# Gated cross-attention and expert FFN on one core: the context tiles of seven batches turned by DMA transposes instead of TensorE

## The chip, the cores and the metric

The kernel runs on one core of a Trainium2 chip. The metric is the device time of one execution in microseconds. A core has TensorE (PE in the profile; PEld is its weight load), VectorE (DVE), ScalarE (ACT), GpSimd (POOL) and SyncE (SP), each with an instruction queue of its own that it works through in order, and 16 DMA engines. An instruction may wait for a semaphore, and then everything behind it on its engine waits as well.

## The reference

x and the context are 8 batches of 512 tokens by 512 features. A layer norm of x, cross-attention with 8 heads of 64 to the context, an output projection with a gate, and after that a second layer norm and a top-2-of-8 expert FFN:

```
q = (x @ Wq).reshape(B, N, NUM_HEADS, HEAD_DIM)...
k = (context @ Wk)...          v = (context @ Wv)...
attn = softmax(einsum('bhnd,bhmd->bhnm', q, k) * scale)
x = x + tanh(g_xattn[0]) * (einsum('bhnm,bhmd->bhnd', attn, v)... @ Wo + bo)
logits = einsum('bnd,de->bne', layernorm(x), gate_w)   # top 2 of 8 experts
x = x + tanh(g_ffn[0]) * (the two experts' FFN, weighted)
```

## The kernel before, in words

**Splits.** Each fp32 operand of a large product is written as two f16 halves, hi and lo, and a product is three f16 matmuls (hi·hi, hi·lo, lo·hi). ScalarE writes hi, VectorE computes operand minus hi and writes lo.

**Steps.** The main loop has 32 steps, `g = 4 * b + j`: batch b, head pair j. In a step TensorE works on the eight score tiles of pair (b, j) (`scores`, k = 0 to 7), the row maxima of the next pair (`row_max_scores`), the q and k projections of the pair after that (`product` of `qk_parts`), the probabilities times V (`weighted`), and, for the batch before, the transposed head outputs (`oT`), the output projection (`out`), the gate logits and the ranks. ScalarE computes each exponential twice, fp32 into `P32` and f16 into `Ph`; the difference `Pl` is made by VectorE (chunks 0 and 1) and by GpSimd (chunks 2 and 3).

**The tiles of the next batch** are prepared beside it. A batch has four tiles of 128 tokens of x and four of the context. In steps j = 0 and j = 1 two of each are turned: ScalarE normalises x into `xn`; `token_tile` has TensorE transpose the x tile and the context tile, in four 128x128 fp32 transposes each, into PSUM; ScalarE reads the bank and writes hi into `xT` or `cT` (`turned_hi`), VectorE writes lo (`turned_lo`). The first of the two tiles of a step (`side(ahead)`) stands between the transposes of oT and `scores` 6, the second (`side(ahead + 1)`) at the very end of the step. In steps j = 2 and j = 3 `side` is the V projection, which reads `cT`, and the k projections from j = 2 on read it as well. The DMAs that load the tiles of batch b + 2 go out from ScalarE's queue in step j = 2 (`load_tile`).

**PSUM.** `bank_uses` lists all uses of shared banks in order, `bank_places` gives each a place: two banks of `G` in turn, or one of the two banks of `MX`, which otherwise hold the row maxima. A use of `G` waits until the last but one use of `G` has been taken out. The first context tile of each step goes into `MX`, and TensorE waits for `mrow_ready` (the max rows copied out of it) before.

**SyncE's queue** in a step: in batch 0 three loads of FFN weight pieces (`load_piece`); the load of the residual (`load_residual`); `arrange`, twelve DMAs that put q and k into the layout for the scores; `max_rows`, two small DMAs which the next step's first scores wait for; in batch 0 three stores of split pieces (`store_piece`); `turn`, two DMA transposes of the finished second-norm row; `store_x2`. ScalarE and VectorE split the pieces in batch 0 (`piece_hi`, `piece_lo`).

## Time and profile before

| | |
|---|---|
| median of 3 timed runs | 1020.25 us (1018.52 to 1021.1) |
| profiled execution | 1017.04 us, span 1015.3 us |
| TensorE busy | 882.5 us, 87% |
| VectorE, ScalarE, GpSimd busy | 689.9, 568.1, 530.5 us |
| TensorE clock granted, mean | 0.96 of full |

The span is the time from the first to the last instruction of the program; the profiled execution's time lies 1.7 us above it. Busy times are unions of an engine's instructions; a matmul's end is modelled, so the distance between the starts of two matmuls says more than their lengths. In a timeline row, `[0.62 <-DVE tiles L974]` means that the engine stood idle for 0.62 us before this instruction and that VectorE's instruction of line 974, which wrote `tiles`, released it. The main loop runs from 50 us to some 730 us; the expert FFN follows.

### The profile page before, as it was taken

Reading aid. Unit: us, or ns where it says so; the run is one execution under the profiler, and the core shown is the slowest. Engines: PE = TensorE matmul, PEld = TensorE weight load, DVE = VectorE, ACT = ScalarE, POOL = GpSimd, SP = SyncE. Lnnn points to the kernel's source line nnn. Section 1 sums busy time; section 2 is a strip of 40 time slices with the busy share of each in tenths; the row PEclk is TensorE's granted clock in tenths of the full one; section 3 lists DMA queues with packets and bytes.
Section 4 is the critical chain, followed back from the end, with each engine's and each line's share of the span. In section 5 each row is a group of like instructions: output and inputs, shape, how many; then the busy total and the mean of one; then the engine's idle time right before and its main releaser. Section 6 shows DMA issues by size and latency. Waiting matters only on the chain. (4 is left out here: it accounts for less than half of the span.)

```text
span 1015.3 us, 22868 instructions
## 1 busy us (share of the span) xinstructions
PE 882.5 (87%) x8250; PEld 536.1 (53%) x8250; DVE 689.9 (68%) x1612; ACT 568.1 (56%) x1022; POOL 530.5 (52%) x643
## 2 busy tenths in 40 slices
PE   4878999999999999999999999997670899899990
PEld 2334555555555555555555555554340678677770
DVE  5577987677877887787787688688466455345540
ACT  4367766567546656755666665566430466456550
POOL 6222253454466456546545654547754155667765
PEclk9999999999999999999999999999885899999995
DMA  7557834645652354355245433753423589899997
GB/s 264 144 152 225 266 119 123 187 118 116 162 158 73 102 166 109 79 157 164 64 118 151 111 77 95 246 180 95 151 95 136 157 183 206 169 215 213 221 170 100
DMA packets 120509, 153.21 MB, mean 151 GB/s; under 512 B 42960, under 2 KB 75728, under 8 KB 119632
## 3 DMA queue, kind: packets, MB, share of 16 engines
q1 hardware_dynamic: 96624, 101.77, 35.2%
q0 software_dynamic: 16864, 37.40, 18.8%
q10 hardware_dynamic: 6912, 12.59, 4.1%
q8 instruction: 69, 1.13, 0.5%
q14 instruction: 40, 0.33, 0.1%
HBM read 67.06 MB, written 56.56 MB: 122 GB/s over the span
## 5 line engine op out<-in xcount | busy, mean ns | idle before, releaser
L700 POOL TENSOR_TENSOR Pl<-P,Ph 128x512 f16<-128x512 f32 x128 | 152.6, 1203 | 167.5 <-ACT Ph L786 167.0
L783 ACT ACTIVATE P<-ST 128x512 f32<-128x512 f32 x256 | 154.5, 603 | 128.9 <-PE ST L1476 109.2
L984 DVE TENSOR_REDUCE mx<-MX 128x1 f32<-128x512 f32 x256 | 168.7, 685 | 27.9 <-PE MX L1461 27.6
L786 ACT ACTIVATE Ph<-ST 128x512 f16<-128x512 f32 x256 | 155.7, 608 | 1.2 <-remote 0.7
L750 POOL DMA_INDIRECT out_dram<-V,Ph x78 | 121.9, 1563 | 62.2 <-ACT V L938 43.7
L1678 PE MATMUL MX<-heads,tiles 128*128 128x256 f16 x936 | 116.8, 276 | 5.7 <-DVE heads L1359 5.4
L1488 PE MATMUL PV<-V,Ph 128*128 128x65 f16 x1024 | 112.0, 194 | 9.8 <-issue 9.6
L1490 PE MATMUL PV<-V,Ph 128*128 128x64 f16 x1024 | 112.2, 195 | 1.8 <-issue 1.8
L1492 PE MATMUL PV<-V,Pl 128*128 128x65 f16 x1024 | 111.8, 193 | 0.7 <-issue 0.6
L1488 PEld LDWEIGHTS PV<-V,Ph 128*128 128x128 f16 x1024 | 96.4, 97 | 29.8 <-issue 11.8
L1490 PEld LDWEIGHTS PV<-V,Ph 128*128 128x128 f16 x1024 | 95.9, 98 | 19.1 <-issue 1.8
L1678 PEld LDWEIGHTS MX<-heads,tiles 128*128 x936 | 90.1, 99 | 26.4 <-issue 9.9
L1475 PE MATMUL ST<-heads 128*128 128x512 f16 x256 | 98.3, 384 | 2.5 <-DMA heads<-mrow 1.2
L1022 DVE TENSOR_TENSOR Pl<-P,Ph 128x512 f16<-128x512 f32 x128 | 99.1, 775 | 0.0
L1476 PE MATMUL ST<-heads 128*128 128x512 f16 x256 | 98.2, 384 | 0.0
L1461 PE MATMUL MX<-heads 128*128 128x512 f16 x256 | 89.3, 383 | 10.1 <-DVE rank_counts L1097 5.1
L1492 PEld LDWEIGHTS PV<-V,Pl 128*128 128x128 f16 x1024 | 96.1, 100 | 1.3 <-issue 1.3
L1414 PE MATMUL G<-tiles,wq_hi 128*128 128x512 f16 x256 | 77.6, 385 | 6.7 <-DVE tiles L974 6.7
L1414 PE MATMUL G<-wv_hi,tiles 128*128 128x512 f16 x256 | 81.7, 379 | 1.4 <-DVE V L1006 1.3
L1414 PE MATMUL G<-tiles,wk_hi 128*128 128x512 f16 x256 | 76.7, 381 | 0.2 <-DVE k_lo L974 0.2
L648 POOL TENSOR_TENSOR second_norm<-second_norm 128x512 f16<-128x512 f32 x29 | 35.0, 1208 | 72.6 <-ACT second_norm L820 72.5
L657 POOL DMA_INDIRECT expert_rows<-second_norm,pos_staged x60 | 60.9, 1014 | 16.2 <-issue 16.0
(261 smaller groups left out, 1880.1 us busy)
## 6 DMA issues: line engine op xcount, KB each, us to landing
heads<-expert_rows SPq DMA_DIRECT2D x39, 516.0 KB
heads<-q_hi SPq DMA_DIRECT2D x124, 64.0 KB, 2.5
heads<-k_hi SPq DMA_DIRECT2D x124, 64.0 KB, 2.9
second_norm<-in_x_dram SPq DMA_DIRECT2D x28, 256.0 KB, 3.1
out_dram<-second_norm SPq DMA_DIRECT2D x28, 256.0 KB, 2.2
tiles<-in_x_dram ACTq DMA_DIRECT2D x24, 256.0 KB, 3.1
tiles<-in_ctx_dram ACTq DMA_DIRECT2D x24, 256.0 KB, 3.9
expert_rows<-zero_rows SPq DMA_DIRECT2D x8, 516.0 KB, 5.6
```

The lines of the kernel that those rows point to most:

```text
L700: nc.gpsimd.tensor_tensor(Pl[:, hh, c, :], P32[:, c, :], Ph[:, hh, c, :], ALU.subtract).then_inc(pl_pool, 1)
L750: nc.gpsimd.indirect_dma_start(out_rows, bass.IndirectOffsetOnAxis(ids[:, s, k:k + 1], 0), y_sb[:, s % YR, k, :], None, compute_op=ALU.add) \
L783: nc.scalar.activation(P32[:, c, :], ST[:, c % 2, :], ACT.Exp, scale=0.125 / SC2).then_inc(p_ready, 1)
L786: nc.scalar.activation(Ph[:, hh, c, :], ST[:, c % 2, :], ACT.Exp, scale=0.125 / SC2).then_inc(ph_ready, 1)
L984: nc.vector.tensor_reduce(out=mx[:, k // TT, k % TT:k % TT + 1], in_=MX[:, (k + odd) % 2, :], axis=AXX, op=ALU.max).then_inc(mx_taken, 1)
L1022: nc.vector.tensor_tensor(Pl[:, hh, c, :], P32[:, c, :], Ph[:, hh, c, :], ALU.subtract).then_inc(pl_vec, 1)
L1414: last = nc.tensor.matmul(out_, a, m, start=(n == 0), stop=(n == len(parts) - 1))
L1475: nc.tensor.matmul(ST[:, c % 2, :], K1[:, j, hh, cols], Q1[:, j, hh, :], start=True, stop=False)
L1488: nc.tensor.matmul(out_[:, 0:HD + 1], Ph[:, hh, c, cols], V[:, r, c, h, 0:HD + 1], start=(c == 0), stop=False)
L1490: nc.tensor.matmul(out_[:, 0:HD], Ph[:, hh, c, cols], V[:, r, c, h, HD + 1:], start=False, stop=False)
L1492: last = nc.tensor.matmul(out_[:, 0:HD + 1], Pl[:, hh, c, cols], V[:, r, c, h, 0:HD + 1], start=False, stop=(c == TT - 1))
L1678: last = nc.tensor.matmul(dst, w, uT[:, s % 2, a, c * UR:(c + 1) * UR], start=k == 0, stop=k == len(parts) - 1)
```

## The change

The context tiles of batches 1 to 7 (28 tiles) are no longer transposed by TensorE. ScalarE writes hi, and VectorE lo, from the loaded tile in its natural layout into `c_split`, which lies over the x tile of the same number (`x_in`, by then normalised). SyncE then issues one DMA transpose for each half, which writes `cT`. Batch 0's context tiles stay as they were. The waits that follow from it: the k projection of step j = 2 waits for all transposes of a batch (`ctx_turned`), and so do the loads of the next tiles into `x_in`; TensorE's waits for the context tile's PSUM banks are gone, and `bank_places` no longer gives them a place.

```diff
-        return tuple([("x", t), ("c", t)] if j < 2 else [("v", t)] for t in tiles)
+        return tuple([("x", t)] if j < 2 else [("v", t)] for t in tiles)
...
-        elif kind == "c" and n >= TT and n % 2 == 0:
-            places[kind, n] = "MX", 1 - g % 2, g
...
+        c_split = slab(0, 2).rearrange("p (t a d) -> p t a d", t=TT, a=2)
...
+            def turn_context(n):
+
+                b, t = divmod(n, TT)
+                if b >= 2:
+                    sp.wait_ge(filled, use["k", 4 * b - 7] + 1)
+                sp.wait_ge(ctx_lo, n - TT + 1)
+                for a in range(2):
+                    sp.dma_start_transpose(cT[b % 2][a][:, :, t * P:(t + 1) * P], c_split[:, t, a]).then_inc(ctx_turned, 16)
...
                 if g >= 5:
                     turn(g - 5)
+                if b < B - 1 and j < 2:
+                    for n in range(2):
+                        turn_context(4 * (b + 1) + 2 * j + n)
                 if b:
                     store_x2(g - 4)
...
+            def context_hi(n):
+
+                t = n % TT
+                act.wait_ge(xn_ready, n + 1)
+                act.wait_ge(c_ld[t], (n // TT + 1) * 16)
+                nc.scalar.activation(c_split[:, t, 0], c_in[:, t, :], ACT.Copy, scale=XS).then_inc(ctx_hi, 1)
...
             def load_tile(b, t):
 
+                act.wait_ge(ctx_turned, (b - 1) * TT * 2 * 16)
...
-                    turned_hi(n) if j < 2 else v_hi(n)
+                    turned_hi(n, "x") if j < 2 else v_hi(n)
...
+                if more and j < 2:
+                    context_hi(ahead)
                 if b == 0:
                     piece_hi(3 * j + 1)
                 exps(hd + 1, 1, 1)
...
+            def context_lo(n):
+                t = n % TT
+                dve.wait_ge(ctx_hi, n - TT + 1)
+                nc.vector.scalar_tensor_tensor(out=c_split[:, t, 1], in0=c_in[:, t, :], scalar=XS, in1=c_split[:, t, 0],
+                                               op0=ALU.mult, op1=ALU.subtract).then_inc(ctx_lo, 1)
...
-                pe.wait_ge(c_ld[n % TT], (n // TT + 1) * 16)
-                transposes(("c", n), c_in[:, n % TT, :])
...
-                if k == 1 and g >= 2 and b < B - 1 and j < 2:
-                    pe.wait_ge(evacuated, use["c", TT * (b + 1) + 2 * j] + 1)
...
+                        if j == 2 and n == "k":
+                            pe.wait_ge(ctx_turned, (b + 1) * TT * 2 * 16)
```

SyncE's queue at the end of batch 0's first step and the start of its second (L446 is `max_rows`, L493 `store_piece`, L488 `load_piece`, L440 `arrange`), before:

```order
L446 DMA heads<-mrow 1x4x128 x2
L493 DMA fu_split<-second_norm 256x1x1024 x2
L493 DMA fu_split<-O 256x1x1024
L488 DMA second_norm<-in_L_ffn_Wu_dram 128x8x128
L488 DMA second_norm<-in_L_ffn_Wv_dram 128x8x128
L488 DMA O<-in_L_ffn_Wv_dram 128x8x128
L440 DMA heads<-q_hi 64x512 x4
```

and now (L486 is `turn_context`):

```order
L446 DMA heads<-mrow 1x4x128 x2
L502 DMA fu_split<-second_norm 256x1x1024 x2
L502 DMA fu_split<-O 256x1x1024
L486 DMA_TRANSPOSE tiles<-tiles 128x4x128 x4
L497 DMA second_norm<-in_L_ffn_Wu_dram 128x8x128
L497 DMA second_norm<-in_L_ffn_Wv_dram 128x8x128
L497 DMA O<-in_L_ffn_Wv_dram 128x8x128
```

Four transposes stand between the stores of one step and the loads of the next.

ScalarE in the second step of a later batch, from k_hi to the second x tile (L783 and L786 are the two exponentials, L817 and L820 the second norm, `tiles<-G` and `tiles<-MX` the hi halves of the x and the context tile), before:

```order
L768 ACTIVATE k_hi<-G 128x512
L783 ACTIVATE P<-ST 128x512
L786 ACTIVATE Ph<-ST 128x512
L817 ACTIVATE second_norm<-second_norm,ln_factors 128x512
L820 ACTIVATE second_norm<-second_norm,ln_factors 128x512
L783 ACTIVATE P<-ST 128x512
L786 ACTIVATE Ph<-ST 128x512
L768 ACTIVATE oT_hi<-MX 128x512
L768 ACTIVATE tiles<-G 128x4x128
L768 ACTIVATE tiles<-MX 128x4x128
```

and now (L816 is `context_hi`):

```order
L780 ACTIVATE k_hi<-G 128x512
L795 ACTIVATE P<-ST 128x512
L798 ACTIVATE Ph<-ST 128x512
L836 ACTIVATE second_norm<-second_norm,ln_factors 128x512
L839 ACTIVATE second_norm<-second_norm,ln_factors 128x512
L816 ACTIVATE tiles<-tiles 128x512
L795 ACTIVATE P<-ST 128x512
L798 ACTIVATE Ph<-ST 128x512
L780 ACTIVATE oT_hi<-MX 128x512
L780 ACTIVATE tiles<-G 128x4x128
L816 ACTIVATE tiles<-tiles 128x512
```

One context split more now stands ahead of oT_hi; the step's second one takes the place of the first one's PSUM read.

VectorE in the same step, from its Pl of the second head to the second x tile, before:

```order
L1022 TENSOR_TENSOR Pl<-P,Ph 128x512
L974 SCALAR_TENSOR_TENSOR oT_lo<-MX,oT_hi 128x512
...
L974 SCALAR_TENSOR_TENSOR tiles<-G,tiles 128x4x128
L974 SCALAR_TENSOR_TENSOR tiles<-MX,tiles 128x4x128
L1022 TENSOR_TENSOR Pl<-P,Ph 128x512
L1035 SCALAR_TENSOR_TENSOR second_norm<-G,gate,second_norm 128x512
...
L1097 COPY rank_counts<-MX 128x40
L974 SCALAR_TENSOR_TENSOR tiles<-G,tiles 128x4x128 x2
```

and now (L1030 is `context_lo`):

```order
L1052 TENSOR_TENSOR Pl<-P,Ph 128x512
L1030 SCALAR_TENSOR_TENSOR tiles<-tiles 128x512
L998 SCALAR_TENSOR_TENSOR oT_lo<-MX,oT_hi 128x512
...
L998 SCALAR_TENSOR_TENSOR tiles<-G,tiles 128x4x128
L1030 SCALAR_TENSOR_TENSOR tiles<-tiles 128x512
L1052 TENSOR_TENSOR Pl<-P,Ph 128x512
L1065 SCALAR_TENSOR_TENSOR second_norm<-G,gate,second_norm 128x512
...
L1127 COPY rank_counts<-MX 128x40
L998 SCALAR_TENSOR_TENSOR tiles<-G,tiles 128x4x128
```

The first split moved ahead of oT_lo, the second one stands ahead of Pl, and one read of PSUM behind the rank counts is gone.

## Rows read from the trace of the kernel before

**Rows 1.** The page, busy us by engine.

```profile
PE 882.5 (87%) x8250; PEld 536.1 (53%) x8250; DVE 689.9 (68%) x1612; ACT 568.1 (56%) x1022; POOL 530.5 (52%) x643
```

**Rows 2.** Windows: second step of batches 0, 2 and 4; length, busy us, clock.

```profile
71.80:92.20 20.40, 17.02 (x161) 10.45 (x162) 16.22 (x28) 15.50 (x28) 5.42 (x5) 0.92 0.69 211
236.80:257.70 20.90, 19.65 (x209) 11.54 (x208) 18.26 (x48) 14.54 (x29) 9.52 (x10) 1.00 0.55 117
412.40:434.30 21.90, 19.79 (x209) 11.66 (x207) 18.28 (x46) 14.92 (x29) 10.39 (x12) 1.00 0.32 80
```

**Rows 3.** Timeline of TensorE, batch 4, first step's end: start us, us, instruction, idle.

```profile
408.18 0.38 PE L1414 MATMUL G<-wo_hi,oT_hi 128*128 128x512 f16 x1 [0.26 <-DVE oT_lo L974]
...
411.97 0.60 PE L1423 MATMUL G<-identity,tiles 128*128 128x128 f32 x4
412.41 0.38 PE L1475 MATMUL ST<-heads 128*128 128x512 f16 x1
...
413.84 0.60 PE L1414 MATMUL G<-tiles,wq_hi 128*128 128x512 f16 x2 [0.62 <-DVE tiles L974]
```

**Rows 4.** Timeline of TensorE, batch 4, end of the second step.

```profile
433.84 0.63 PE L1423 MATMUL G<-identity,tiles 128*128 128x128 f32 x4 [0.80 <-DVE second_norm L1035]
...
435.41 0.38 PE L1461 MATMUL MX<-heads 128*128 128x512 f16 x1 [0.52 <-DVE rank_counts L1097]
```

**Rows 5.** Timeline of ScalarE, batch 4, first step.

```profile
406.68 0.63 ACT L768 ACTIVATE oT_hi<-MX 128x512 f16<-128x512 f32 x1
407.15 0.64 ACT L768 ACTIVATE tiles<-G 128x512 f16<-128x512 f32 x1
...
412.17 1.08 ACT L768 ACTIVATE tiles<-G 128x512 f16<-128x512 f32 x2 [1.94 <-PE G L1423]
```

**Rows 6.** Timeline of VectorE, batch 4, second step.

```profile
430.41 0.68 DVE L974 SCALAR_TENSOR_TENSOR tiles<-MX,tiles 128x512 f16<-128x512 f32 x1
431.01 2.02 DVE L1022 TENSOR_TENSOR Pl<-P,Ph 128x512 f16<-128x512 f32 x1
...
435.08 0.19 DVE L1097 COPY rank_counts<-MX 128x40 f32<-128x40 f32 x1
```

**Rows 7.** Timeline of GpSimd, the same place.

```profile
430.19 2.28 POOL L700 TENSOR_TENSOR Pl<-P,Ph 128x512 f16<-128x512 f32 x2
```

**Rows 8.** Timeline of SyncE's queue, batch 4, first step's end.

```profile
410.22 2.52 SPq L477 DMA_TRANSPOSE second_norm<-second_norm  x2
...
413.47 0.37 SPq L453 DMA_DIRECT2D second_norm<-in_x_dram  x1
419.50 2.44 SPq L440 DMA_DIRECT2D heads<-q_hi  x4
```

**Rows 9.** List of DMA issues: count, KB each, median us to landing.

```profile
second_norm<-in_x_dram SPq DMA_DIRECT2D x28, 256.0 KB, 3.1
...
second_norm<-in_L_ffn_Wu_dram SPq DMA_DIRECT2D x3, 512.0 KB, 5.2
```

**Rows 10.** Timeline of TensorE, batch 4, second step: first P·V of its first head.

```profile
426.59 0.19 PE L1488 MATMUL PV<-V,Ph 128*128 128x65 f16 x1
```

**Rows 11.** Timeline of SyncE's queue, batch 0, first and second step.

```profile
69.29 1.31 SPq L446 DMA_DIRECT2D heads<-mrow  x2
...
73.78 0.37 SPq L488 DMA_DIRECT2D second_norm<-in_L_ffn_Wu_dram  x1
...
88.75 1.29 SPq L446 DMA_DIRECT2D heads<-mrow  x2
```

**Rows 12.** Timeline of ScalarE, batch 0, second step: the hi half of a piece.

```profile
81.35 1.06 ACT L834 ACTIVATE second_norm<-second_norm 128x1024 f16<-128x1024 f32 x1
```

**Rows 13.** Timeline of TensorE, batch 0, second step.

```profile
71.80 0.39 PE L1475 MATMUL ST<-heads 128*128 128x512 f16 x1 [0.90 <-DMA heads<-mrow]
...
87.04 1.09 PE L1423 MATMUL MX<-identity,tiles 128*128 128x128 f32 x4 [2.82 <-DVE mrow L994]
```

**Rows 14.** Timeline of ScalarE, batch 4, third step.

```profile
440.25 0.60 ACT L768 ACTIVATE q_hi<-G 128x512 f16<-128x512 f32 x1 [1.01 <-PE G L1414]
```

More of the change, by code:

```diff
@@ L102, in bank_places @@
     for kind, n in uses:
-        g = n + 4 if kind == "oT" else 4 * (n // TT - 1) + n % TT // 2
+        g = n + 4
         if kind == "ranks" and 4 * n + 9 < steps:
@@ L324, in layer @@
         c_ld = [sem(f"ctx_loaded{t}") for t in range(TT)]
+        ctx_hi, ctx_lo = sem("ctx_hi_written"), sem("ctx_lo_written")
+        ctx_turned = sem("ctx_parts_turned")
         ln_ready = sem("ln_factors_ready")
@@ L566, in step @@
                     sp.wait_ge(filled, use["k", g - 1] + 1)
-                    sp.wait_ge(filled, use["c", TILES - 1] + 1)
+                    sp.wait_ge(ctx_turned, (B - 1) * TT * 2 * 16)
                     for k in range(3):
@@ L903, in step @@
                     side(ahead)
+                    if j < 2:
+                        context_hi(ahead + 1)
                 exps(hd + 1, 1, 2)
@@ L1273, in side @@
                 def side(n):
-                    turned_lo(n) if j < 2 else v_lo(n)
+                    turned_lo(n, "x") if j < 2 else v_lo(n)
                 maxima(0, 1, 2, 3)
@@ L1299, in step @@
                     piece_lo(3 * j + 1)
+                if more and j < 2:
+                    context_lo(ahead)
                 if b:
@@ L1309, in step @@
                     side(ahead)
+                    if j < 2:
+                        context_lo(ahead + 1)
                 if j == 3 and b < B - 2:
@@ L1403, in bank @@
                     pe.wait_ge(evacuated, use[since_] + 1)
-                elif name[0] == "oT":
+                else:
                     pe.wait_ge(mx_taken, min(since_ + 2, STEPS) * 2 * TT)
-                else:
-                    pe.wait_ge(mrow_ready, since_ + 2)
                 return MX[:, k, :]
@@ L1601, in step @@
                         dst = bank((n, g))
-                        if j == 2:
-                            pe.wait_ge(evacuated, use["x" if n == "q" else "c", TT * (b + 2) - 1] + 1)
+                        if j == 2 and n == "q":
+                            pe.wait_ge(evacuated, use["x", TT * (b + 2) - 1] + 1)
+                        if j == 2 and n == "k":
+                            pe.wait_ge(ctx_turned, (b + 1) * TT * 2 * 16)
                         product(dst, parts[n], 0, 6)
```

## Prediction

> **What bounds the kernel now.** I read the page's busy times first: TensorE is busy for 87% of the span [rows 1]. Then the windows, one for each step of the main loop: in the second step of batch 4 TensorE works 19.79 of 21.90 us at full clock [rows 2]. So in the loop a TensorE microsecond is worth a microsecond where TensorE is not made to wait, and the short waits decide. I took these from TensorE's timeline around the transposes that go away. There are four in a batch. In the first two steps the out-projection waits for VectorE's low half of oT (0.26 us in the first [rows 3]). At the change from the first to the second step, the q projection waits 0.62 us for the low half of the last x tile, whose PSUM bank it needs [rows 3]. At the end of the second step the context transpose waits 0.80 us for VectorE's x2 row to leave its bank, and the row-max matmul behind it waits 0.52 us for VectorE to take the rank counts [rows 4]. Behind the oT wait stands ScalarE: it runs without a pause from k_hi to the exponentials of the step's last score tiles and rests only then, 1.94 us [rows 5]. Behind the rank wait stands VectorE: its Pl subtraction took 2.02 us instead of some 0.68 because GpSimd's two Pl subtractions ran from 430.19 for 2.28 us [rows 6, 7].
>
> **What goes.** 28 tiles, four fp32 transposes each. One tile costs 412.41 - 411.97 = 0.44 us of TensorE [rows 3], so 28 x 0.44 = 12.3 us of work, and with the waits of 0.80 some 15 us at most. Each step loses one transpose in front of its out-projection and one behind it.
>
> **First step of a batch (six times, batches 1 to 6).** ScalarE now splits the first context tile before it comes to the second exponentials and oT_hi. The split reads SBUF and writes f16; I price it as the row for the same Copy from PSUM, start to start 407.15 - 406.68 = 0.47 [rows 5]. ScalarE is what oT waits for, so oT_lo and the out-projection move from 408.18 to about 408.68. The 0.44 saved ahead of it only lengthens that wait. Behind it TensorE saves the second 0.44, and the next step begins at 412.45, not 412.41: nothing so far. But the PSUM rotation changes: with no context tile, the q projection of the second step takes the bank of the out-projection, whose reader is done, and not that of the x tile. It starts some 0.7 us after the scores and not 1.43 us (413.84 - 412.41 [rows 3]). Gain 0.7 each, 4.2 us in all if the second steps leave it standing. VectorE must follow: its work there is unchanged in amount and one split has moved into a pause.
>
> **Second step.** Measured from the same clock, all is 0.7 earlier at first, then ScalarE's split puts oT 0.5 back. TensorE alone would reach the end 0.44 + 0.80 + 0.4 earlier. But VectorE sets it. It reaches the second context split at 430.2 (now 430.41, less 0.7, plus 0.5), and that op then reads two SBUF operands, where the old one read PSUM [rows 6]. GpSimd's Pl pair, now at 430.19, comes 0.5 to 0.7 earlier as well, at about 429.65, and runs 2.3 us [rows 7], so the split waits until 431.95, as the Pl in [rows 6] did, and the Pl follows only at 432.6. Pl now ends at 433.2 (before: 433.03) and the ranks come 0.2 later than before, so the row maxima start at 435.6 against 435.41 [rows 4]. The pair of steps loses 0.2 where it had gained 0.7. That holds for batches 3 to 6: +0.8 us. In batch 2 this step took 20.90 us, not 21.90 [rows 2]: no such collision now, so there the new one costs a further 1.0: +1.2. Batch 1 has no ranks; I take the gain of the first step less a part of a collision: -0.3. Sum +1.7 us; without any collision it would be -7 (1.5 for each of four, 1 for batch 1).
>
> **The queue of SyncE.** Each of the 14 steps puts four transposes on it. The two there now take 2.52 us to issue [rows 8], so 5.0 us more. In batch 4 the queue is idle from 413.84 to 419.50 [rows 8]: they fit, with 0.6 us left. Behind them wait the x2 store and the residual load, 5 us later; GpSimd's bias add waits for the load, then come its Pl parts. The load lands 3.1 us after issue [rows 9], at 421.6, the add and two Pl parts of some 1.2 us each end at 425.3, and TensorE, which takes them at 426.59 now [rows 10], needs them at 425.9. Cost zero, and if the load takes 1 us longer, 0.4 us in six steps.
>
> **Batch 0** is where they don't fit. Here the queue also loads the FFN weight pieces. The load at 73.78 [rows 11] now stands behind four transposes: it goes out at 79.4 (5.0 for the queue, 0.6 because the piece store ahead waits for VectorE, which has one more split before it). It lands 5.2 us later [rows 9], at 84.6, and ScalarE wants the piece at 81.35 [rows 12], some 0.4 earlier now. Stall 3.2 to 3.6 us. Behind it in ScalarE's order: the x tiles, k_hi, all exponentials; behind k_hi the twelve arranging DMAs and the max rows, issued at 88.75 for 1.29 us [rows 11]. These go to about 92. The scores of the next step waited for that DMA until 71.80 one step before, 1.2 us after its issue ended (69.29 + 1.31 [rows 11, 13]). So the next step starts at 94.4, not 92.20 [rows 2]: +2.2 us. The wait of 2.82 us on mrow [rows 13] goes away, but TensorE then waits for the late exponentials in its place; the like wait in the first step goes too, and there the DMA of 71.80 holds the gain back [rows 13]. In the third step the same happens to the next pieces, which ScalarE wants later in its step; I take a third of it, 0.8 us (0 to 2.2). Together +3.0 us, between -1 (the loads land as fast as the best) and +5.
>
> **Sum.** +1.7 + 3.0 = +4.7 us. The profiled execution took 1017.04 us (span 1015.3), 3.2 below the median of the three timed runs, 1020.25. On the profile that is 1021.7, on the median **1025.0 us**. A measurement of this kernel tells about 0.3%, 3 us, from no change.
>
> **How long a transpose takes to land** no row shows. From below it is its issue, 1.26 us; from above the 256 KB load, 3.1, or the 512 KB piece, 5.2 [rows 9]. It moves 128 KB, so I take 2.5. The last one of a batch is then in place at 438.1, and ScalarE, which may load the next tiles only then, needs its place in the queue by q_hi at 440.25 [rows 14].
> The Trainium skill (VectorE: DVE Perf Modes, The three transpose paths and Rules for kernel authors) gives 1309 ns for a 128x128 transpose by DMA against 390 ns on TensorE, and advises TensorE where PSUM will do. Four blocks one after another would be 5.2 us for a tile half, an estimate from that page, and with it the change is slower by the third rival below. The issue rows here show all four blocks taken in 1.26 us.
>
> **Rivals.**
> *The collision does not come* (faster). VectorE's second split starts before GpSimd's first Pl part; it needs 0.55 us for that, and it decides everything. Then each of batches 3 to 6 gains 1.5, batch 1 gains 1, and with batch 0 as above the sum is -7 + 3 = -4.0: **1016.3 us**; with batch 0 without cost 1012. For it: in the first step the Pl started just ahead of GpSimd's, and 15 us of work and waits do go. Against: the oT chain puts VectorE later, not earlier. Chance 0.27. The Trainium skill (SBUF — State Buffer, Who interferes with whom) says that of such a pair the one issued first keeps the shared port for the whole instruction; the 2.02 us row agrees, and by it the rival hangs on that half microsecond.
> *Batch 0 hides it* (no change). The pieces land before ScalarE wants them: +1.7 alone, **1022.0 us**. Against it: 3 us are missing. Chance 0.20.
> *The turned tiles land late* (much slower). At 5.2 us instead of 2.5 ScalarE's wait ahead of q_hi costs up to 2.7 less the 2 us to spare, and the arranging DMAs behind the transposes as much again; at the worst 2.7 in six steps on top: 16 us, **1041 us**. The decision point is a landing of 4.5 us. Chance 0.08.
> My forecast has 0.45; the lower end of its own range (1022 to 1028) reads as no change.
>
> **Range and chances.** 1013 takes in most of the first rival, 1031 the upper bound of batch 0 (+2) with the residual load (+2.4) and a first step whose gain is eaten by a collision (+1.5); only the late landing and the best of the first rival stay out, under 2 in 10. Faster 0.27, same 0.20 + 0.05 = 0.25, slower 0.40 + 0.08 = 0.48.
>
> **What the new profile would show.** The waits for x (0.62) and for the x2 row (0.80) gone; the oT waits of first and second steps above 1 us; the context split at 2 us in second steps, and the rank wait grown to about 2 us; q projection 0.7 us after the scores; the first piece of batch 0's second step waited for by ScalarE for 3 us and the third step starting near 94.4; SyncE without idle time in first and second steps. I am wrong if the split takes its 0.7 us in the second steps, if the oT wait does not grow, or if the piece is there in time.

## Result and the profile after

The changed kernel takes 1036.24 us (median of 4 runs, 1034.91 to 1038.04), the kernel before 1020.1 in the same sitting: ratio 1.016, interval 1.014 to 1.018. It is 16.1 us slower. The forecast was slower, 1025.0, range 1013 to 1031: the sign was right, the size three times too small and the range missed. The profiled execution is the slowest of the four: 1038.04 us, span 1036.3. The kernel before was profiled in an execution of 1017.04 us, below its median, so the two traces lie 21.0 us apart and not 16.1; what is counted by steps below adds up to some 21.

The page after, against [rows 1]:

```profile
PE 883.2 (85%) x8138; PEld 530.5 (51%) x8138; DVE 704.6 (68%) x1612; ACT 570.9 (55%) x1022; POOL 538.5 (52%) x643
```

112 TensorE instructions are gone, and TensorE is as busy as before. The windows say why. They are the second and third step of batch 0, the third of batch 2, the three first steps of batch 4 and the first of batch 7 (length, then busy us of PE, PEld, DVE, ACT, POOL with counts, clock, DMA share, GB/s):

```profile
72.41:95.38 22.97, 17.67 (x154) 10.08 (x154) 16.90 (x28) 16.10 (x29) 6.51 (x5) 0.85 0.66 195
95.38:120.14 24.76, 20.86 (x170) 10.19 (x170) 16.42 (x27) 13.80 (x24) 7.72 (x6) 0.93 0.94 299
268.01:292.53 24.52, 22.77 (x203) 11.91 (x201) 19.43 (x52) 12.63 (x23) 12.38 (x14) 1.00 0.71 189
404.48:424.30 19.82, 18.28 (x186) 10.50 (x185) 15.40 (x26) 14.52 (x27) 12.82 (x18) 1.00 0.27 65
424.30:444.50 20.20, 18.45 (x202) 10.85 (x200) 18.20 (x44) 14.62 (x28) 11.02 (x12) 1.00 0.48 103
444.50:470.49 25.99, 23.87 (x203) 12.43 (x201) 19.90 (x46) 12.63 (x23) 11.26 (x14) 0.93 0.67 183
674.46:696.12 21.66, 18.81 (x179) 9.99 (x178) 12.92 (x22) 12.04 (x22) 10.77 (x12) 0.92 0.57 177
```

The second step of batch 4 fell from 21.90 us [rows 2] to 20.20, and TensorE works 1.34 us less in it. The third step then took 25.99 us at a mean clock of 0.93. TensorE's timeline where the second step passes into the third:

```profile
444.71 0.38 PE L1504 MATMUL ST<-heads 128*128 128x512 f16 x1
447.21 0.38 PE L1489 MATMUL MX<-heads 128*128 128x512 f16 x1 [2.12 <-DVE rank_counts L1127]
...
447.81 0.59 PE L1446 MATMUL G<-tiles,wq_hi 128*128 128x512 f16 x2
...
448.45 1.06 PE L1446 MATMUL G<-tiles,wq_hi 128*128 128x512 f16 x2
```

The reader is to see two things. The wait for the rank counts is 2.12 us where it was 0.52 [rows 4]: what the second step saved is waited away here. And 1.2 us later the same two matmuls take 1.06 us and not 0.59: from 448.45 to 451.86 the granted clock stands at 0.5, that is 1.2 instead of 2.4 GHz. Between 100 and 690 us the trace before has no such stretch; this one has four (from 260.71, 448.45, 537.19 and 629.35, each 3.41 us). The last three begin at the end of a rank wait or just behind it; the first begins inside another wait, that of P·V in the second step of batch 2. Each costs half its length, 1.7 us, of TensorE's work. In time it costs some 1.4 us: with the rank wait of 2.12 us as the only idle time of TensorE above 0.2 us, the third step of batch 4 took 25.99 us here and 24.63 us at full clock in changed_again, a second trace of this kernel. (Batch 3's took 25.99 us here too, at full clock, but with two more waits, 0.54 and 0.51 us.)

Behind the wait stands the chain that was forecast, VectorE and GpSimd in the same step:

```profile
441.96 1.29 DVE L1030 SCALAR_TENSOR_TENSOR tiles<-tiles 128x512 f16<-128x512 f32 x1
443.18 1.65 DVE L1052 TENSOR_TENSOR Pl<-P,Ph 128x512 f16<-128x512 f32 x1
...
446.88 0.19 DVE L1127 COPY rank_counts<-MX 128x40 f32<-128x40 f32 x1
```

```profile
441.54 2.73 POOL L712 TENSOR_TENSOR Pl<-P,Ph 128x512 f16<-128x512 f32 x2
```

In batch 0, SyncE's queue and ScalarE:

```profile
74.14 6.23 SPq L486 DMA_TRANSPOSE tiles<-tiles  x4
80.43 0.57 SPq L497 DMA_DIRECT2D second_norm<-in_L_ffn_Wu_dram  x1
...
97.79 5.72 SPq L486 DMA_TRANSPOSE tiles<-tiles  x4
103.55 1.21 SPq L497 DMA_DIRECT2D second_norm<-in_L_ffn_Wv_dram  x2
```

```profile
84.75 1.06 ACT L854 ACTIVATE second_norm<-second_norm 128x1024 f16<-128x1024 f32 x1 [3.26 <-DMA second_norm<-in_L_ffn_Wu_dram]
...
104.75 0.45 ACTq L844 DMA_DIRECT2D tiles<-in_x_dram  x1
105.24 0.45 ACTq L845 DMA_DIRECT2D tiles<-in_ctx_dram  x1
105.78 0.60 ACT L780 ACTIVATE q_hi<-G 128x512 f16<-128x512 f32 x1 [3.29 <-issue]
```

The piece that left at 73.78 before [rows 11] leaves at 80.43, and ScalarE waits 3.26 us for it. In the third step ScalarE stands again, 3.29 us: the loads of batch 2's tiles, which may start only when the turned tiles have landed, stand ahead of q_hi in its order.

**Where the time went.** From the starts of the steps (first ST matmul) in both traces, the changed kernel falls behind by 7.1 us in batch 0, 0.9 in batch 1, 2.3, 1.2, 2.0, 1.5 and 3.0 in batches 2 to 6, and 3.3 in the first step of batch 7.

### The profile page after: what moved, and what is told of

Read it like the earlier page. It is cut to its first block, busy times and chain, and to the rows that moved or that the text cites. A ratio compares the mean times of both kernels' runs of the same rounds, so it can differ in the third digit from the quotient of the medians.

```text
span 1036.3 us, 22710 instructions
## 1 busy us (share of the span) xinstructions
PE 883.2 (85%) x8138; PEld 530.5 (51%) x8138; DVE 704.6 (68%) x1612; ACT 570.9 (55%) x1022; POOL 538.5 (52%) x643
## 4 chain that ended last, share of the span: by engine, by line
PE 49%; DVE 15%; ACT 10%; DMA 10%; issue 7%; SPq 4%; POOL 2%; another core or an unknown queue 1%; ACTq 0%; POOLq 0%; DVEq 0%
PE G L1446 23%; DMA out_dram<-V,Ph 7%; PE MX L1708 5%; PE MX L1489 4%; PE ST L1504 3%; PE ST L1503 3%; DVE Pl L1052 2%; ACT Ph L798 2%; PE G L1700 2%; PE PV L1516 2%; DVE mx L1008 2%; PE PV L1518 2%; PE PV L1520 2%; SPq L440 2%; POOL out_dram L762 1%
## 5 line engine op out<-in xcount | busy, mean ns | idle before, releaser
L712 POOL TENSOR_TENSOR Pl<-P,Ph 128x512 f16<-128x512 f32 x128 | 158.2, 1249 | 136.4 <-ACT Ph L798 136.0
L1516 PEld LDWEIGHTS PV<-V,Ph 128*128 128x128 f16 x1024 | 97.5, 98 | 39.1 <-issue 22.0
L1503 PE MATMUL ST<-heads 128*128 128x512 f16 x256 | 99.6, 389 | 15.6 <-ACT Ph L798 10.8
L1489 PE MATMUL MX<-heads 128*128 128x512 f16 x256 | 91.4, 391 | 19.1 <-DVE rank_counts L1127 12.3
L1518 PEld LDWEIGHTS PV<-V,Ph 128*128 128x128 f16 x1024 | 97.0, 99 | 18.5 <-issue 1.9
L1504 PE MATMUL ST<-heads 128*128 128x512 f16 x256 | 99.4, 388 | 0.0
L651 POOL TENSOR_TENSOR second_norm<-second_norm,tgbo 128x512 f32<-128x512 f32 x28 | 36.6, 1309 | 108.7 <-DMA second_norm<-in_x_dram 108.7
L1446 PE MATMUL G<-tiles,wq_hi 128*128 128x512 f16 x256 | 80.9, 399 | 2.8 <-DVE tiles L998 2.8
L669 POOL DMA_INDIRECT expert_rows<-second_norm,pos_staged x60 | 61.2, 1020 | 16.2 <-issue 16.1
```

The costliest lines, as they stand in the source:

```text
L712: nc.gpsimd.tensor_tensor(Pl[:, hh, c, :], P32[:, c, :], Ph[:, hh, c, :], ALU.subtract).then_inc(pl_pool, 1)
L1446: last = nc.tensor.matmul(out_, a, m, start=(n == 0), stop=(n == len(parts) - 1))
L1489: nc.tensor.matmul(MX[:, (k + g) % 2, :], Q1[:, s, h, t * P:(t + 1) * P], K1[:, s, h, :], start=True, stop=True).then_inc(mx_filled, 1)
L1503: nc.tensor.matmul(ST[:, c % 2, :], K1[:, j, hh, cols], Q1[:, j, hh, :], start=True, stop=False)
L1516: nc.tensor.matmul(out_[:, 0:HD + 1], Ph[:, hh, c, cols], V[:, r, c, h, 0:HD + 1], start=(c == 0), stop=False)
L1518: nc.tensor.matmul(out_[:, 0:HD], Ph[:, hh, c, cols], V[:, r, c, h, HD + 1:], start=False, stop=False)
```

## Experiments

Theory 1: batch 0's queue, with the price of the transposes in it. Theory 2: in second steps VectorE's and GpSimd's chain holds the end fixed, so that TensorE's saving turns into a wait, and the clock falls behind that wait. Rival to both: transposes cost the same wherever they stand, by landing late or taking bandwidth. The kernel before took 1019 to 1021 us in most sittings, but 1008 to 1009 in the two of residual_early, pieces_first, per_tile and filled_wait, and of copies, product_first, b2_on_product_first and j0_residual_early. So every kernel is given as its ratio to the kernel before in its own sitting. The fourth steps of batches 2 to 5 take 22.0 us in the traces of those two sittings and 22.9 to 25.4 in all others, whichever the kernel, so single steps are compared within a sitting where that can be done.

### Which tiles cost

The set of tiles that the DMA turns became a function; all others go the old way, waits, banks and splits included.

```
+def by_dma(n):
+    return n >= 8                      # b0_old
+    return n >= 8 and n % 4 < 2        # b0_old_j0: first steps only
+    return n >= 8 and n % 4 >= 2       # b0_old_j1: second steps only
```

> Batch 0's four context tiles (those of batch 1) go back to TensorE, the other 24 stay with the DMA. If batch 0 lost its 7.4 us to its own queue (the next weight piece and the loads of batch 2 stand behind the four transposes), the time is 1036.2 - 7 = about 1029 us, and the starts of batch 1 stand as before the change. If the loss is spread, because transposes land late everywhere, at most 3 us come back and the time is 1033 or more.

> Batch 0 the old way, and of the later batches only the tiles of the first steps by DMA (12 tiles). Theory (the cost lies in the second steps, where VectorE's split collides with GpSimd ahead of the rank counts and the granted clock falls after the wait): no stretch at half clock between 100 and 690 us, 1019 to 1022 us. Rival (every transpose costs, wherever it stands, by the SP queue and late landings): half of b0_old's remaining loss, 1024 to 1025 us.

> Batch 0 the old way, and of the later batches only the tiles of the second steps by DMA (12 tiles). Theory (collision and clock in the second steps): TensorE waits about 2 us for the rank counts in batches 2 to 6, a stretch at half clock follows in most of them, 1026 to 1029 us. Rival (cost by the number of transposes): 1024 to 1025 us.

Measured: b0_old 1028.2 us, ratio 1.006 (1.003 to 1.009): of the 16 us, 8 (by the times) to 10 (by the ratios) lie in batch 0. b0_old_j0 1018.8, ratio 0.998 (0.996 to 1.000), no stretch at half clock between 100 and 690 us. b0_old_j1 1031.9, ratio 1.009 (1.006 to 1.013). The twelve tiles of the second steps cost 9 us (by the ratio) to 11 (by the times) and the twelve of the first steps none; a price by the number of transposes is out. The second steps' loss is larger than expected, and only in part where theory 2 has it: in b0_old_j1's profile the rank wait is 2.12 us in batches 3 to 6, but second and third step together are only 0.2 to 1.0 us longer than before there and 2.6 and 2.7 us longer in batches 1 and 2, and the clock falls once (260.41). The fourth steps of batches 4 to 6 take 24.3 to 25.4 us instead of 22.6 to 23.3, with row maxima that wait up to 2.1 us for VectorE. That trace of the kernel before is from another sitting; in b0_old_j0, of the same one, they take 23.4 to 24.2. Why they are longer is not settled.

### The order on VectorE

```
                     side(ahead)
-                    if j < 2:
+                    if j == 0 or j == 1 and b < 2:
                         context_lo(ahead + 1)
...
                     take_ranks(b - 2)
+                    if more:
+                        context_lo(ahead + 1)
```

> All 28 tiles by DMA; in the second steps of batches 2 to 6 VectorE splits the second context tile behind its copy of the rank counts, not ahead of it. Theory: the wait for the rank counts shrinks from 2.1 us to 0.6 or less, and the stretches at half clock behind it go too (1.7 us each): 5 x (1.5 + 1.7) = 16 us at most, 8 to 12 us likely, so 1024 to 1028 us. Rival (the clock falls for another reason, or the wait only moves to the next product): 1033 us or more, with the stretches still there.

Measured: 1033.9 us, ratio 1.012 (1.009 to 1.015). The rival's side. VectorE in batch 3:

```profile
354.98 2.61 DVE L1052 TENSOR_TENSOR Pl<-P,Ph 128x512 f16<-128x512 f32 x1
...
359.64 0.19 DVE L1127 COPY rank_counts<-MX 128x40 f32<-128x40 f32 x1
```

The split is out of the way, and Pl now stands the time that the split stood. The end is the same: in the kernel before ([rows 6, 7]), in the changed kernel and here, Pl ends 0.56 us behind GpSimd's pair, with one or two operations of VectorE beside the pair. The rank wait was 1.87 us, and four stretches at half clock remain between 100 and 690 us. The chain is bound by GpSimd's pair, not by the number of VectorE's operations in front of it. That corrects theory 2: the collision is not added by the change, it is [rows 6] in another place. Here Pl was issued 0.2 us behind the first of GpSimd's pair and ended 0.6 us behind the second. The Trainium skill (SBUF — State Buffer, Who interferes with whom) says that the instruction which has the shared port keeps it to its end; this row agrees.

### The wait and the clock

Nine matmuls of 512 columns into the bank of the coming q product, whose results are written over:

```
                     scores(b, j, k)
+                    if j == 2 and 2 <= b < B - 1 and k == 0:
+                        junk = bank(("q", g))
+                        for _ in range(9):
+                            nc.tensor.matmul(junk, K1[:, j, 0, 0:P], Q1[:, j, 0, :], start=True, stop=True)
                     maxima(2 * k)
```

> All 28 tiles by DMA; in the third steps of batches 2 to 6 nine matmuls of 512 columns, about 2.0 us, whose results are written over, stand ahead of the row maxima that wait 2.1 us for the rank counts. Theory (TensorE's idle time there brings the stretches at half clock): no such stretch between 255 and 650 us, each saves 1.3 to 1.7 us, 4 to 6 us in all less the overhang of the filler (0.3 us each): 1031 to 1033 us. Rival (the stretches have another cause): they stay, 1036 to 1038 us.

Measured: ratio 1.011 (1.007 to 1.015), some 5 us better than the changed kernel's 1.016 (the intervals just overlap) by doing useless work. The windows of the third steps of batches 3, 4 and 5:

```profile
358.60:383.99 25.39, 24.47 (x212) 12.82 (x210) 20.37 (x49) 12.64 (x23) 10.67 (x14) 1.00 0.68 189
447.71:471.98 24.27, 24.13 (x212) 12.84 (x210) 18.35 (x44) 12.63 (x23) 10.70 (x14) 1.00 0.68 188
534.04:559.38 25.34, 24.30 (x212) 12.74 (x210) 20.35 (x48) 12.63 (x23) 10.86 (x14) 1.00 0.70 184
```

Full clock in all three; in per_tile, in the same sitting, these steps took 26.71, 26.14 and 26.00 us. Behind the rank wait no stretch is left. The row maximum starts 0.4 us behind the rank counts in batches 3, 5 and 6 and 1.4 behind them in batches 2 and 4, where the filler is longer than the wait. Elsewhere the stretches stay: one from 261.39 in a second step whose P·V waits 4.4 us, one from 442.29 behind two waits of 1.05 and 0.69 us in batch 4's second step, which took 21.87 us for it and not 20.19. With the second steps counted, the filler gained 1.3, 0.2, 0.6 and 1.4 us in batches 3 to 6. A waiting TensorE brings the fall, but not each time: in b0_old the same wait of 2.12 us in batches 4 to 6 had full clock.

Useful work in the same place, the last head's first part and half of the q product:

```
-                    maxima(2 * k)
+                    late = j == 2 and k == 0 and 2 <= b < B - 1
+                    if not late:
+                        maxima(2 * k)
...
                         product(dst, parts[n], 0, 6)
+                    if late:
+                        maxima(0)
```

> All 28 tiles by DMA; in the third steps of batches 2 to 6 TensorE does a part of the last head and the first half of the q projection ahead of the row maximum that waits for the rank counts. Theory: 1.5 to 2 us of useful work fill the wait of 2.1 us and no stretch at half clock follows it: 5 x (1.2 to 1.6 + up to 1.4) us = 6 to 12 us less than the changed kernel, ratio 1.004 to 1.010. Rival (second and third steps are bound by VectorE's and GpSimd's chain, so that work done early only makes another wait later in the third step): second and third step together stay at 45 us or more, ratio 1.011 to 1.016.

Measured: ratio 1.020 (1.016 to 1.023), no gain, and above what either side expected. TensorE in batch 3:

```profile
359.90 0.59 PE L1446 MATMUL G<-tiles,wq_hi 128*128 128x512 f16 x2 [2.38 <-DVE tiles L998]
```

The product needs the x tile's low half, which VectorE takes right behind the rank counts. The wait changed its name and grew.

### SyncE's queue

```
                     turn(g - 5)
+                if 4 <= g < STEPS - 4:
+                    load_residual(g - 3)   # residual_early; no longer at the next step's start
                 if b < B - 1 and j < 2:
```

```
+                if g < 2:                  # pieces_first; no longer at the next step's start
+                    for i in range(3 * j + 3, 3 * j + 6):
+                        load_piece(i)
                 if b < B - 1 and j < 2:
```

> All 28 tiles by DMA; only the residual load of the next step goes into SyncE's queue ahead of this step's four context transposes, not behind them. Theory (the queue makes the residual, GpSimd's add and its pairs of probabilities late): add_bias starts as early in its step as before the change, the late steps (first step of batch 7, 21.66 us, third step of batch 6) go back to 18.4 and 24.7 us, 4 to 6 us less in all: 1030 to 1032 us. Rival (the lateness is covered or moves to the transposes): 1035 us or more.

> All 28 tiles by DMA; in batch 0 the loads of the next step's three weight pieces stand in SyncE's queue ahead of the four transposes. Theory (the 8 us of batch 0 are the pieces' place behind 6 us of transposes, plus the loads of batch 2 that wait for the turned tiles): the second and third steps get shorter by 2 to 5 us together, 1031 to 1034 us. Rival (contention of the transposes with other transfers, whatever the order): the start of batch 1 is moved by less than 1 us, 1035 to 1037 us.

Measured: residual_early ratio 1.0135 (1.011 to 1.016) against 1.016: some 2.6 us better, less than the 4 to 6 expected, and the intervals overlap. What it mends shows in the trace of the changed kernel, second step of batch 2, queue and then GpSimd and TensorE:

```profile
247.03 5.14 SPq L486 DMA_TRANSPOSE tiles<-tiles  x4
252.21 1.74 SPq L466 DMA_DIRECT2D out_dram<-second_norm  x1
254.05 0.38 SPq L453 DMA_DIRECT2D second_norm<-in_x_dram  x1
```

```profile
256.92 1.27 POOL L651 TENSOR_TENSOR second_norm<-second_norm,tgbo 128x512 f32<-128x512 f32 x1 [9.39 <-DMA second_norm<-in_x_dram]
258.14 3.25 POOL L712 TENSOR_TENSOR Pl<-P,Ph 128x512 f16<-128x512 f32 x2
```

```profile
261.49 0.21 PE L1516 MATMUL PV<-V,Ph 128*128 128x65 f16 x1 [3.34 <-issue]
```

The residual left 8.8 us into the step, GpSimd idled 9.39 us for it, its pair ended at 261.39 and TensorE's P·V, held 3.34 us, began 0.1 us later. With the load early that step took 20.45 us (24.90 in filled_wait of the same sitting) and the first step of batch 7 18.38 (21.65). But in batch 2 the third step grew to 28.18 us: its k product waits 1.51 us for the turned tiles, now behind the load.

pieces_first came out at 1.025 (1.022 to 1.028), worse than the changed kernel. The third step of batch 0 took 30.62 us, at a mean clock of 0.78. TensorE at the start and in the middle of the third step:

```profile
94.17 0.61 PE L1506 MATMUL ST<-heads 128*128 128x512 f16 x1 [6.55 <-DMA heads<-mrow]
108.63 1.01 PE L1449 MATMUL G<-tiles,wk_hi 128*128 128x512 f16 x2 [7.03 <-DMA tiles<-tiles]
```

A piece may load only when the piece before it in its buffer is stored, so the queue stood for the stores with the transposes behind it. The expectation was wrong in its sign; the queue of batch 0 is full whatever the order.

```
-                act.wait_ge(ctx_turned, (b - 1) * TT * 2 * 16)
+                act.wait_ge(ctx_turned[t], (b - 1) * 2 * 16)
```

> All 28 tiles by DMA; the loads that fill a tile's buffer again wait for that tile's own transposes, not for all four tiles of the batch. Theory: in the third steps of batches 0 and 1 ScalarE no longer waits 3.3 us ahead of the q parts, TensorE's wait for the turned tiles stays, 1 to 3 us less than the changed kernel: 1033 to 1035 us. Rival (the wait was covered): 1036 us.

Measured: ratio 1.018 (1.015 to 1.021), no gain. ScalarE's wait ahead of q_hi fell from 3.29 to 1.31 us and TensorE's for the turned tiles rose from 0.82 to 1.80: the loads' wait was covered by that of the transposes, as the rival had it.

### The price of turning

```
-                    sp.dma_start_transpose(cT[b % 2][a][:, :, t * P:(t + 1) * P], c_split[:, t, a])
+                    sp.dma_start(cT[b % 2][a][:, :, t * P:(t + 1) * P],
+                                 c_split[:, t, a].rearrange("p (c n) -> p c n", c=KC))
```

In copies for all tiles, in copies_b0 for those that batch 0 prepares.

> All 28 tiles; each transpose from SyncE is replaced by a plain DMA of the same 128 KB from the same rows to the same place in runs of 256 bytes, so nothing is turned and the output's numbers are others (the time is what is asked for). Theory (a large part of the cost is the 1.25 to 1.5 us for which each of the 56 transposes holds SyncE's queue, in batch 0 above all): the queue is free sooner, the second and third steps of batch 0 lose at least 3 us, the residual loads come 3 us earlier, ratio to the kernel before 1.003 to 1.009. Rival (the cost is the bytes and the order of work on ScalarE, VectorE and GpSimd): ratio 1.013 or more, like the changed kernel's 1.016.

> The changed kernel with plain copies in place of the eight transposes of batch 0 alone (nothing turned there, the output's numbers are others), the 48 later transposes stay. Theory (in batch 0 the queue is full, later it has room): batch 1 starts 2.5 to 4 us sooner than in the changed kernel, and that is all: ratio 0.0025 to 0.004 below that of changed_again. Rival (transposes cost as much later): batch 0 gives under 1 us, the rest of the difference to the copies lies behind it.

> The changed kernel once more, for a trace on the same chip as the others of this call. Ratio 1.014 to 1.018. If its loop loses more than copies' did by batch 7's first step, the difference is the price of transposing as such.

> The kernel before once more, for its trace on this chip: ratio 1.000, within 0.003; its loop is the scale for the steps of the others, and on a chip of 1008 us its fourth steps take 22.0 us where those of the chip of 1020 us took 22.6 to 23.3.

Measured: copies 1.0025 (1.0004 to 1.0045); copies_b0 1.011 (1.008 to 1.014); changed_again 1.017 (1.014 to 1.020); before_again 0.9995. The last three share a chip, so steps can be compared. Second and third step of batch 0 in before_again, in changed_again and in copies_b0:

```profile
72.40:91.16 18.76, 15.71 (x161) 9.29 (x162) 15.69 (x26) 14.67 (x27) 4.64 (x4) 1.00 0.71 211
91.16:112.38 21.22, 19.26 (x169) 9.88 (x169) 18.39 (x29) 13.81 (x26) 6.34 (x5) 1.00 1.00 318
```

```profile
73.74:96.05 22.31, 16.75 (x154) 8.91 (x154) 16.08 (x28) 15.22 (x27) 5.79 (x4) 0.92 0.68 201
96.04:120.64 24.60, 20.98 (x169) 10.22 (x169) 16.57 (x27) 14.03 (x24) 7.97 (x6) 0.93 0.95 298
```

```profile
72.51:92.69 20.18, 16.91 (x153) 9.70 (x153) 16.46 (x28) 15.68 (x29) 6.07 (x4) 0.86 0.74 222
92.70:114.88 22.18, 20.18 (x170) 9.75 (x170) 16.58 (x26) 13.53 (x23) 7.79 (x6) 0.97 1.03 323
```

The two steps take 39.98, 46.91 and 42.36 us: of 6.9 us lost, 4.5 come back with the copies (expected 2.5 to 4). The queue, changed_again and then copies_b0:

```profile
74.84 6.73 SPq L486 DMA_TRANSPOSE tiles<-tiles  x4
...
98.71 5.39 SPq L486 DMA_TRANSPOSE tiles<-tiles  x4
```

```profile
74.16 3.71 SPq L487 DMA_DIRECT2D tiles<-tiles  x4
...
95.46 2.81 SPq L487 DMA_DIRECT2D tiles<-tiles  x4
```

Four transposes hold the queue 3.0 and 2.6 us longer than four copies of the same bytes, 5.6 us in all, and the loop gets 4.5 us back: in batch 0 a microsecond of the queue is nearly one of the kernel. The rest, 2.4 us, stays with copies too: splits, loads, the place in the queue, and 6.8 us at half clock, which both these kernels have in the two steps and before_again has not. Over all traces, batch 0 takes 79.9 to 83.2 us with its tiles on TensorE, 83.8 and 85.4 with copies and 86.5 to 90.0 with transposes (93.4 in pieces_first). In landing there is no difference; the list of DMA issues has, for the changed kernel and for copies (median us to landing last):

```profile
tiles<-tiles SPq DMA_TRANSPOSE x56, 2.5
```

```profile
tiles<-tiles SPq DMA_DIRECT2D x56, 128.0 KB, 2.6
```

The Trainium skill (Advanced Engine Details and Errata, X-Bar Transpose) says that transposing DMAs are as fast as plain ones; for the landing this trace agrees, for the issue it does not.

copies gained more than batch 0 explains, and came out below what was expected (1.003 to 1.009). How much of that is the transposes' price behind batch 0 stays open: since nothing is turned, the numbers and with them the experts' routing are others, and behind the loop its profile is 4.0 to 4.5 us shorter than the others of its sitting. In batches 3 to 5 its second and third steps show no gain: together 46.3 to 46.9 us (46.2 to 46.4 in the changed kernel, in another sitting), with a rank wait of 2.1 to 2.4 us and a stretch at half clock in each.

In before_again and changed_again the loss by batch is 8.5, 1.3, 2.5, 0.0, 0.2, 3.5, 1.5 and, in the first step of batch 7, 2.8 us. Batches 3 and 4 had full clock throughout here, and cost nothing; batch 5 holds 6.83 us at half clock. Of the 8.5 us, 1.9 lie in batch 0's first step, which takes 20.2 to 23.0 us even among the kernels whose batch 0 is the old one.

### A version that beats the kernel before

> Batch 0 the old way, the tiles of batches 2 to 7 by DMA, residual loads ahead of the transposes, product ahead of the waiting row maximum. If the mends add up (batch 0 -8 us, late residuals -4, rank wait and clock -6 or more): ratio 0.996 to 1.000, no slower than the kernel before. Rival (first and second steps have nothing to gain from a freer TensorE): 1.002 to 1.006.

> Twelve tiles, those of the first steps from batch 2 on, by DMA, and the residual loads ahead of the transposes. Theory: as with these twelve tiles alone, less the wait of 1.2 us in the first step of batch 7: ratio 0.995 to 0.999. Rival (early residual loads move GpSimd's add into another pair of VectorE): 1.000 or more.

> The kernel before, no tile by DMA, with the residual load of the next step issued one step earlier. If the gain of the mended version is owed to the twelve tiles, this is 1.000 within 0.002; if to the residual loads, it is 0.995 to 0.997.

b2_on_product_first joins b0_old, residual_early and product_first: ratio 1.012 (1.008 to 1.016), where 0.996 to 1.000 or, by the rival, 1.002 to 1.006 was expected. Its third steps of batches 2 to 6 still take 26.3 to 27.5 us, with a stretch at half clock in each. j0_residual_early joins b0_old_j0 and the early residual load: 0.995 (0.993 to 0.997). before_residual_early, the same load order without any tile by DMA, is 1.000 (0.998 to 1.002): the gain needs the tiles.

> The same kernel as j0_residual_early, run again. If its gain is the kernel's: ratio 0.993 to 0.997. If it was that chip's: 0.998 to 1.001.

> As j0_residual_early, with the split of the first context tile behind the parts of oT on ScalarE and VectorE. Theory (the first step's waits for oT_lo and Ph come from the split ahead of them): the step takes 19.0 to 19.3 us instead of 19.82, six times, ratio 0.003 to 0.005 below that of j0_residual_early2. Rival (the attention rows are held by something else, GpSimd's pair of probabilities for one): 19.8 us, same ratio within 0.002.

```
+                if more and j < 2 and by_dma(ahead):
+                    context_hi(ahead)      # behind hi_part(("oT", g - 4), ...), not ahead of it
...
+                if more and j < 2 and by_dma(ahead):
+                    context_lo(ahead)      # behind lo_part(("oT", g - 4), ...)
```

j0_residual_early2 on another chip again 0.995 (0.991 to 0.998); j0_oT_first 0.993 (0.990 to 0.995), 1014.5 against 1021.5 us, the fastest of all. First and second step of batch 4 in the former, and in the latter:

```profile
390.06:409.88 19.82, 18.29 (x186) 10.49 (x185) 15.05 (x26) 14.51 (x27) 13.82 (x21) 1.00 0.21 49
409.88:430.96 21.08, 19.60 (x209) 11.75 (x207) 18.14 (x45) 14.65 (x28) 10.36 (x12) 1.00 0.47 111
```

```profile
391.93:411.24 19.31, 18.11 (x186) 10.42 (x185) 14.41 (x26) 14.52 (x27) 13.07 (x21) 1.00 0.19 46
411.25:432.33 21.08, 19.58 (x210) 11.71 (x207) 18.53 (x45) 14.66 (x28) 10.96 (x13) 1.00 0.48 112
```

The second step is 0.8 us shorter than in [rows 2], with no tile of its own changed: the bank rotation's gain (the wait of 0.62 in [rows 3] is gone) stands here, GpSimd's pair and the rank counts come 0.8 us earlier in the step as well. With a second split in front of Pl, the changed kernel had its rank counts 22.76 us into the step, the kernel before 22.86, this one 22.05. The first step is 0.5 us shorter with the splits behind oT; the wait for Ph is gone, that for oT_lo (0.69) is not. So the split ahead of oT cost 0.5 us, and the oT wait itself has another cause. By the ratios the gain is 0.002 (0.003 to 0.005 expected), and the two kernels' intervals overlap.

## Why the forecast was wrong

**First steps: right.** The step was to grow by 0.04 us in batch 4; it took 19.82 against 19.75. The oT wait grew from 0.26 to 0.70, and a new wait of 0.34 for Ph stands before it: together the 1 us named. The q product of the second step starts 0.65 us after the scores (0.7 forecast), and the waits of 0.62 and 0.80 are gone.

**Second steps: right in time and mechanism, blind to what follows.** From the start of the first step to the row maximum behind the rank counts: 42.75 us before, 42.73 after (forecast +0.2). The rank wait is 2.1 us as forecast, the split took 1.29 and not 2 us, with Pl at 1.65. The step that failed is the sum that ended there: it priced the wait of 2 us at what it delays, and left out what TensorE's clock does after it. Three stretches at half clock stand behind it here, some 1.4 us each, 4 us together. filled_wait shows these to hang on the rank wait; in changed_again batches 3 and 4, with the wait and without them, cost 0.0 and 0.2. That a fall comes in some batches and not in others with the same wait is not explained, nor is the rest of the second steps' loss in b0_old_j1.

**The queue.** "Cost zero" for the late residual load was wrong in batch 2: the sum used batch 4's queue, where the load left 6.1 us into the step (measured 6.24) and GpSimd was in time. In batch 2 two stores of zero rows and a late x2 store stand in the same queue, it left after 8.8 us, and P·V waited 3.34. In batch 6's second step it left after 7.2 us, P·V waited 0.92, and the step took 21.73 us and not 20.19. The four transposes took 5.14 us at best and 5.4 to 6.7 in batch 0, not 5.0. In batch 7's first step GpSimd had the residual 2.2 us later than before and P·V waited 2.85 us, though the load left at the same place in the step; beside it run two loads of 1 MB. That wait comes in some kernels and not in others, and copies has it as well; its cause is open. It is absent with early residual loads, but also in ranks_first and per_tile, which load late.

Batch 1, forecast at -0.3, lost 0.9 and 1.3: its third step, not thought of, waits for the turned tiles too.

**Batch 0: 3.0 forecast, 7.1 and 8.5 in two pairs of traces.** The second step's part was right: stall 3.26 (3.2 to 3.6), third step at 95.38 (94.4), +2.6 us (+2.2). The term mis-sized is "I take a third of it, 0.8 us" for the third step: it took 24.76 us instead of 20.44. There the next four transposes hold the queue 5.72 us, the pieces leave at 103.55, and a stretch at half clock lies in it. The guard against late landing was made for batch 4's q_hi; in batch 0 the turned tiles are the last thing in a full queue and k waits for them.

**Landing.** 2.5 us was assumed and 2.5 is the median, 4.8 the longest; from batch 2 on TensorE never waits for the turned tiles. The rival of late landing does not hold, though its time, 1041, is nearer than the forecast's. "The collision does not come" and "batch 0 hides it" are refuted by the rows above.

**The range** failed because two separate prices were missed and both lie on the same side: the clock was left out, and the full queue was put at its low end in batch 0 and at nothing in batches 2 and 6.

## What to carry to other kernels

Work taken off the busiest engine is worth something only in a step whose end that engine sets; where another chain sets it, the saving turns into idle time of TensorE, and that can cost more than it hides. Sort a change's sites by that before making it: here the same edit was worth 0.2% at twelve sites (an interval that reaches no change), 0.5 to 0.7% with the residual loads and the splits moved as well, and lost at the other sixteen. Price a queue stage by stage: transposes that fit into a gap in one batch stand in front of everything in another.

## What the runs showed of the hardware

A DMA transpose of 128x512 f16, four in a row, held SyncE's queue 1.3 to 1.7 us and a plain DMA of the same 128 KB 0.7 to 0.9, with the same landing of 2.5 and 2.6 us. With waits of TensorE of 2.1 to 3.3 us the granted clock fell to 1.2 GHz in some batches and stayed at 2.4 in others; in eight of the traces it also fell behind the two waits of a second step (0.9 to 1.5 us for Ph, 0.7 for oT_lo), which in most batches were followed by full clock. Useless matmuls in the rank wait left no fall behind it and made the kernel some 0.5% faster (1.011 against 1.016, intervals that just overlap). GpSimd's pair of subtractions stretched whichever VectorE operation with two SBUF operands it met, up to 2.7 us (a context split in changed_again) for one that takes 0.68 alone.
